# Attention stage of a two-layer block: scores ahead of the output projection on TensorE, mask ahead of the row update on VectorE, query/key projection moved by half a slot

## The reference, cut to what matters

```
q = phi(x @ W_q);  k = phi(x @ W_k);  v = x @ W_v          # phi(a) = elu(a) + 1
S = S + k_t v_t^T;  z = z + k_t                             # running state over tokens
o_t = (S q_t) / max(z . q_t, 1e-6)
x = x + o @ W_o
```

## Time and profile before

| | |
|---|---|
| time, median of 3 runs | 298.87 us (298.55 to 299.95) |
| the profiled execution: its own time | 298.89 us |
| its span, first to last instruction | 297.2 us |
| mean granted TensorE clock | 0.994 of full speed |
| TensorE matmul busy | 277.5 us, 93% of the span |
| VectorE busy | 239.7 us, 81% |
| ScalarE busy | 183.0 us, 62% |
| GpSimd busy | 225.2 us, 76% |

### The profile page before, as it was taken

One profiled execution on the slowest core, in us unless ns is written; L12 is line 12 of the kernel. 1 busy time (PEld: TensorE's weight loads), 2 busy tenths in 40 slices (PEclk: granted clock), 3 DMA queues, 4 the chain that ended last, 5 costly groups with the idle time before them and its releaser, 6 DMA issues.

```text
span 297.2 us, 7729 instructions
## 1 busy us (share of the span) xinstructions
PE 277.5 (93%) x2179; PEld 241.6 (81%) x2179; DVE 239.7 (81%) x1031; ACT 183.0 (62%) x543; POOL 225.2 (76%) x300
## 2 busy tenths in 40 slices
PE   7989999987899999999999989998799999999994
PEld 7556676664499999999995578877689999999994
DVE  4889899999777797777771999888988998877773
ACT  2865666540399877666660477653369986666661
POOL 3967378888768888888652658787578888888874
PEclk9999999999799999999999999999999999999999
DMA  6999800001331453432102700111142444432110
GB/s 177 246 350 223 106 30 31 27 27 38 84 85 47 121 131 88 111 93 67 38 16 77 207 2 1 36 40 46 57 101 62 104 111 94 110 91 76 57 42 3
DMA packets 32521, 25.64 MB, mean 86 GB/s; under 512 B 6000, under 2 KB 28785, under 8 KB 32480
## 3 DMA queue, kind: packets, MB, share of 16 engines
q1 hardware_dynamic: 27328, 16.51, 24.0%
q0 software_dynamic: 4576, 8.54, 8.8%
q10 hardware_dynamic: 576, 0.10, 0.2%
HBM read 14.57 MB, written 11.53 MB: 88 GB/s over the span
## 4 chain that ended last, share of the span: by engine, by line
PE 61%; DVE 22%; POOL 9%; issue 4%; DMA 3%; ACT 1%; DVEq 0%; ACTq 0%; POOLq 0%; SPq 0%
PE pair L1656 22%; PE pair L1642 16%; PE bank L1642 7%; POOL sorted L514 4%; DVE stats L829 3%; PE bank L1632 3%; DVE zT L1069 2%; PE bank L1527 2%; POOL rows L488 2%; DVE rows L971 2%; DVE mv L834 1%; PE pair L1514 1%; PE pair L1481 1%; DVE qk L1062 1%; DVE sc L1128 1%
## 5 line engine op out<-in xcount | busy, mean ns | idle before, releaser
L1656 PE MATMUL pair<-w2s,hT 128*128 x624 | 82.6, 276 | 0.0
L514 POOL DMA_INDIRECT sorted<-rows,place x64 | 64.5, 1008 | 18.7 <-issue 14.8
L1656 PEld LDWEIGHTS pair<-w2s,hT 128*128 128x128 f32 x624 | 75.6, 192 | 0.3
L1642 PE MATMUL pair<-xsT,w1s 128*128 128x128 f32 x432 | 59.9, 276 | 0.9 <-ACT xsT L768 0.9
L1642 PEld LDWEIGHTS pair<-xsT,w1s 128*128 128x128 f32 x432 | 53.8, 192 | 2.0 <-issue 1.0
L691 ACT COPY w1s<-w1all 128x516 f32 x78 | 49.5, 636 | 3.4 <-DVE etab L1211 2.5
L534 POOL DMA_INDIRECT x_mid<-ys,xs x39 | 39.2, 1005 | 12.2 <-DVE ys L1283 7.0
L768 ACT COPY xsT<-bank 128x128 f32<-128x128 f32 x78 | 20.8, 267 | 41.3 <-PE bank L1632 40.4
L534 POOL DMA_INDIRECT out<-ys,xs x39 | 38.8, 996 | 9.6 <-issue 7.1
L1283 DVE SCALAR_TENSOR_TENSOR ys<-pair,xs 128x128 f32<-128x128 f32 x78 | 27.2, 348 | 21.9 <-PE pair L1656 21.7
L1273 DVE TENSOR_SCALAR hT<-pair,w1s 128x128 f32<-128x128 f32 x112 | 34.4, 346 | 1.3
(11 more groups left out here) (172 smaller groups left out, 527.0 us busy)
## 6 DMA issues: line engine op xcount, KB each, us to landing
xs<-sorted SPq DMA_DIRECT2D x78, 66.0 KB, 1.9
w1all<-in_L_ffn_W_b SPq DMA_DIRECT2D x8, 258.0 KB, 5.9
rows<-in_L_attn_a_x SPq DMA_DIRECT2D x8, 256.0 KB, 4.0
w2s<-in_L_ffn_W SPq DMA_DIRECT2D x8, 256.0 KB, 6.1
rows<-x_mid SPq DMA_DIRECT2D x8, 256.0 KB, 4.7
sorted<-pad SPq DMA_DIRECT2D x30, 66.0 KB, 3.0
sorted<-rows,place POOLq DMA_INDIRECT x64, 2.4
x_mid<-ys,xs POOLq DMA_INDIRECT x39, 2.4
```

The costliest lines, as they stand in the source:

```text
L514: pool.indirect_dma_start(sorted_rows[l], bass.IndirectOffsetOnAxis(ap=place[:, t:t + 1], axis=0), rows[:, t, :], None).then_inc(s_sent[l] ...
L1642: mm = nc.tensor.matmul(bank[2 + 2 * half + i % 2][:, c * P:(c + 1) * P], w1s[i % NW][:, f:f + P], xsT[i % NB][:], start=True, stop=True)
L1656: mm = nc.tensor.matmul(bank[6 + i % 2][:, 0:P], hT[i % NB][:, c], w2s[:, bass.ds(e, 1), c, :].rearrange("p o d -> p (o d)"), start=(c == ...
```

## The change

In TensorE's slot, `score_and_turn(k - 1)` stands ahead of `project_out(k - 2)`, and `project_qk` is no longer the first call of its slot: the projection of group k + 1 is made in slot k, between `updates_and_intra(k - 1)` and `read_inter(k - 1)`. In VectorE's slot, `mask_scores(k - 1)` stands ahead of `add_attention(k - 2)`. ScalarE, GpSimd and SyncE are untouched, and so are all waits.

```diff
@@ VectorE
             def attn_slot(k):
 
+                if 0 <= k - 1:
+                    mask_scores(k - 1)
                 if 0 <= k - 2:
                     add_attention(k - 2)
-                if 0 <= k - 1:
-                    mask_scores(k - 1)
@@ TensorE
             def attn_slot(k):
-                if k < NG:
-                    project_qk(k)
+                if k == 0:
+                    project_qk(0)
+                if 0 <= k - 1:
+                    score_and_turn(k - 1)
                 if k - 2 >= 0:
                     project_out(k - 2)
-                if 0 <= k - 1:
-                    score_and_turn(k - 1)
                 if k == 0:
                     turn_output_weights()
                 if k + 1 < NG:
@@
                 if 0 <= k - 1:
                     updates_and_intra(k - 1)
+                if k + 1 < NG:
+                    project_qk(k + 1)
                 if 0 <= k - 1:
                     read_inter(k - 1)
```

## The result

The changed kernel takes 312.13 us (median of 4 runs, 311.19 to 315.12) beside 298.71 for the kernel before: ratio 1.045, 95% interval 1.041 to 1.049, a loss of 13.4 us where 5.5 were forecast. The profiled execution took 311.36 us with a span of 309.6, 12.4 more than the 297.2 of before. All engines have the same instructions. VectorE and ScalarE take the same time for them within 1 us, and GpSimd 221.1 us where it took 225.2; TensorE's busy time grew from 277.5 to 286.1 us.

A forecast was written before the change was run, and what follows sets the result against it. TensorE (busy 34.79 of 37.10 us) and VectorE (33.55) were both taken as close to full. Six slots of 8.2 us give +4.8, read-out 0 +0.3, slot 1 +0.4: 298.9 + 5.5 = 304.4 us, range 302.0 to 306.8.

The forecast's parts named there:

- Filled stalls: TensorE's read-out waits for state (groups 0 to 5) and the 0.8 us of mask waits go: up to 3.0 us gained.
- The wait for `rel`: First transpose into bank 1 waits for ScalarE's copy, `ex`, `rl`: 1.35 us, 1.2 in slots 4 to 7, 1.75 in slot 2.
- The new period, 8.2 us: Attention slot from one `rel` to the next: 8.08 through TensorE, 8.31 through VectorE, taken as 8.2 against 7.41 us.
- the seam terms: Additions outside the six periods: +0.3 us ahead of the read-out of group 0, +0.4 for two small exponentials in slot 1.
- the rival of the falling clock: TensorE idles 1.2 of 8.2 us per attention slot, so its clock halves; two slots cost 14 us, giving 318; 4%.
- the forecast's own sign of being wrong: Wrong if `ex` precedes the copy's end by over 0.1, period is under 7.8, or granted clock is 0.5 in these slots.
- The last slot, "0": Read-out 6 to 7 is VectorE's row update, mask and slot table without a gap; order doesn't matter: 0 us change.
- The handover, "a later end moves everything": Behind attention TensorE is the chain (output projection, clock-keeping matmuls 4.27 us, first expert transpose); all rows 5 to 6 us later.
- The rival "smaller loss" (302.0): ScalarE less late, `ex` following the copy more tightly: period 7.8, a loss of 3.1 us, 302.0 us; 12%.
- The faster rival: Transposes into bank 1 don't wait and filled stalls count: slot about 7.15, 1.6 us gained, 297.3 us; 4%.

## Why the prediction was wrong

The direction was right, and so was the mechanism of the stall; the sum put the fall of the clock behind it at nothing, and that was a term of 7.7 us.

*Filled stalls: right.* The waits for state (groups 0 to 5) and mask are gone. Group 6 was forecast to wait 1.3 us: 1.25 in the kernel with two extra matmuls, but 0.51 in the changed one, where TensorE came later at the lower clock.

*The wait for `rel`: right in place, number and size.* Six waits, 1.69 in slot 2, 1.23 in slot 3, 1.02 in slots 4 to 7, against 1.75, 1.35 and 1.2. Two steps in it were off and offset each other: `rel` came 0.2 later than worked out (copy to `ex` 0.60, not 0.50, and 0.15 behind `rl`, not 0.05), and the scores ahead of the wait took 0.71, not 0.40 (30.00 to 30.71).

*The new period, 8.2 us: nearly right at full clock.* The kernel with two extra matmuls shows 8.33, which is the forecast's own sum through VectorE, 8.31, before it took 0.1 off. That its 304.0 us lie so near to 304.4 is partly luck: five slots were 0.65 longer in all than forecast, and the last slot 1.0 shorter (below). VectorE's waits in it are as forecast too, 0.3 to 0.4 for the scores (1.8 in slot 3) and 0.7 for the output projection; in the changed kernel the second is 1.2 to 1.9. The bounds "303.2 to 306.4" don't follow from the periods beside them: 8.05 and 8.35 with the seam terms give 303.5 and 305.3.

*The step that failed is the rival of the falling clock*: "at 210 to 214 it idled 1.45 of 4.00 us and the granted clock stayed 1.00", hence 4%, priced at 318 and left outside the range, and nothing for the clock in the sum. One stretch, with one stall of 1.13 us in it, was taken as proof for six. In the changed kernel the clock fell behind five of the six stalls, which is the forecast's own sign of being wrong ("if the granted clock is 0.5 in these slots"). The price was off as well: not two whole slots at half clock (14 us) but 7.7 us over five, 1.5 each. The Trainium skill, "TensorE: Matmul & The Clock Gate", section "A second HAM failure mode", says of another kernel that frequent short idles between groups of matmuls make the clock swing between its levels. The trace after agrees, 0.83 mean in five slots against 1.00; those of the kernels with the mask alone and without the early projection don't, as they kept 1.00 in slots with stalls of 0.6 to 1.2 us.

*Where the 12.4 us of the profiled executions are.* Read-out 1 is 1.57 later (28.98 against 27.41; 1.5 was forecast: +0.3, +0.4 and one slot's +0.8). From there to read-out 6, 49.32 against 36.99 (78.30 - 28.98, 64.40 - 27.41): +12.33. Five slots of the kernel with two extra matmuls last 41.64 (28.82 to 70.46), so 4.65 of it is the longer order and 7.68 the clock. Sum 13.90 at read-out 6. The last slot gives back 1.01 and the handover to the experts 0.6; that leaves the 12.3 by which the first tile's second product is late (96.49 against 84.19), and the span grew by 12.4.

*The last slot, "0": wrong by 1.0.* In it VectorE's first step of the slot table, 8 numbers, took 1.24 us before (see the last section) and 0.16 after. That this makes the 1.0 is argued; in the kernel with the early projection alone the step took 0.21, and the slot was 0.6 shorter than before (7.23 against 7.87). *The handover, "a later end moves everything": nearly.* The clock-keeping matmuls took 2.74 us instead of 4.43, as the clock did not fall before them, and 1.1 of the 1.7 were lost again to VectorE's routing:

```profile
89.26 2.74 PE L1527 MATMUL bank<-w2s,ident 128*128 128x512 f32 x6
91.84 0.28 PE L1634 MATMUL bank<-ident,xsn 128*128 128x128 f32 x1
...
96.49 1.15 PE L1658 MATMUL pair<-w2s,hT 128*128 x8 [0.40 <-issue]
```

*The rival "smaller loss" (302.0)* did not come: `ex` followed the copy less tightly than forecast, not more. That the kernel with `ex` and `rl` read ahead takes 301.8 is another mechanism with the same number. *The faster rival* did not come: even with no wait for `rel` and undisturbed slots of 7.0 us the order gave 301.1, with clock stretches in it.

What stays open: why the clock falls behind five stalls of 1.0 to 1.2 us in the changed kernel and not behind its longest, 1.69, nor behind its wait of 1.79 us at 86 to 88; why not behind those of 1.0 to 1.2 in the kernel with the mask alone, nor with two stalls a slot in the kernel without the early projection; and why it did once behind 0.56. The runs show that in the changed kernel the falls hang on the open stalls, and that leaving 0.3 to 1.0 us of each was harmless; they don't show what else decides, and no length of stall parts the two cases.

## What to carry to other kernels

When a call is moved ahead of the work that used to stand between a buffer's readers and its next writer, look at the list of the engine that reads: the reader's place in its own list sets when the buffer is free, not the time at which its input is ready. A stall on TensorE had two prices here, its length and, often, a stretch at the lower clock behind it; where a change puts a stall of about 1 us into every round of a loop, price both, and give the second a real share of the range. Where such a stall can't be removed, a few matmuls without use in it are the cheap repair: here two per slot gave back 8 of 13 us. Reading the bank ahead of the copy, which removes most of the stall, gave back 10.

## What the runs showed of the hardware

The granted clock fell to 0.50 behind a stall and came back while TensorE ran on; in that stretch the output projection took 1.92 us against 1.03. Extra matmuls in the stall kept it at 1.00 in these slots; the same matmuls 1 to 1.7 us behind the end of the stall did not.

A VectorE instruction on 8 numbers took 1.24 us in the kernel before; here it is with what GpSimd did at that time:

```profile
69.75 1.24 DVE L1194 SCALAR_TENSOR_TENSOR ntile<-posb,whole 1x8 f32<-1x8 f32 x1
...
69.68 1.28 POOL L496 TENSOR_TENSOR op<-zT,qk 64x512 f32<-64x512 f32 x1
```

It ended 0.03 us after GpSimd's. In the changed kernel it took 0.16 us and started 0.06 us behind the end of GpSimd's. In the kernel with ScalarE's reads ahead and two buffers it started at 72.83, 0.34 us ahead of that end (71.89 + 1.28 = 73.17), took 0.36 us, and ended 0.02 us behind it. So in these three kernels it ends 0.16 us behind its start or just behind GpSimd's instruction, whichever is later; no run was made for it alone. The Trainium skill, "SBUF — State Buffer", section "SBUF: two separate sides", describes a pair of ports that VectorE (with two inputs from SBUF) and GpSimd can hold only one at a time, each for a whole instruction; the rows agree.
